# Adding expert rows to their tokens in DRAM instead of gathering them back, in a two-layer adaLN block on one Trainium2 core

## What is computed

```python
# layer 0, mixture of experts (E = 64, TOP_K = 8, SEL_K = 4)
top_val, top_idx = top_k(softmax(x @ gate_weight.T), TOP_K)
top_val = top_val / top_val.sum(-1)
mapping = where(replace, best_primary, arange(E))   # merges secondary experts
rerouted = mapping[top_idx]
rerouted[:, :SEL_K] = top_idx[:, :SEL_K]
y = silu(gate) * up @ down            # per expert, rows of its tokens
out = zeros.at[tok].add(y * w)        # back to the tokens
x = x + gb * out
# layer 1, attention (16 heads, 4 kv heads, window 128, 16 meta keys)
h = layernorm(x) * (1 + ca) + sa
x = x + ga * attention(h)
```

## Time and profile before

| | us |
|---|---|
| median of 3 runs (lowest, highest) | 2322.02 (2320.09, 2323.6) |
| the profiled execution, device time | 2322.45 |
| its span in the profile | 2320.6 |
| PE busy | 2024.3 (87%) |
| DVE busy | 1095.3 (47%) |
| ACT busy | 742.9 (32%) |
| POOL busy | 725.6 (31%) |
| mean granted TensorE clock | 0.935 |
| HBM read, written | 216.47 MB, 83.36 MB |

### The profile page before, as it was taken

The page is one execution under the profiler, slowest core; times in us unless marked ns, Lnnn a source line. Parts: engine busy times, 40 slices in busy tenths (PEclk is TensorE's granted clock), DMA queues, the critical chain, the costliest instruction groups (busy, mean ns, idle before and its releaser), DMA issues. The chain is left out here.

```text
span 2320.6 us, 38481 instructions
## 1 busy us (share of the span) xinstructions
PE 2024.3 (87%) x11149; PEld 1332.4 (57%) x11150; DVE 1095.3 (47%) x2952; ACT 742.9 (32%) x1743; POOL 725.6 (31%) x1163
## 2 busy tenths in 40 slices
PE   4799867999999999999971588888866999999998
PEld 2667534555555555555531255555545878878787
DVE  2467667555553222222114577777634444443432
ACT  0233226222222222222210255555642333222322
POOL 0243311222333333333226677777402101011000
PEclk7799879999999999999985689999987999999999
DMA  6556632565555656656625222223011112121210
GB/s 239 177 211 219 235 116 65 182 214 180 190 182 196 193 191 211 215 195 199 213 94 147 82 82 76 83 79 85 5 43 40 64 55 82 64 81 63 73 64 28
DMA packets 122554, 302.32 MB, mean 130 GB/s; under 512 B 24912, under 2 KB 28624, under 8 KB 122320
## 3 DMA queue, kind: packets, MB, share of 16 engines
q1 hardware_dynamic: 73424, 179.04, 22.7%
q0 software_dynamic: 23040, 75.52, 11.4%
q10 hardware_dynamic: 25984, 46.38, 5.3%
HBM read 216.47 MB, written 83.36 MB: 129 GB/s over the span
## 5 line engine op out<-in xcount | busy, mean ns | idle before, releaser
L1166 PE MATMUL bank<-arena 128*128 x1272 | 445.5, 493 | 10.3 <-issue 9.2
L1166 PEld LDWEIGHTS bank<-arena 128*128 128x128 f32 x1272 | 229.6, 190 | 147.7 <-issue 16.9
L1183 PE MATMUL bank<-arena 96*128 x632 | 297.5, 593 | 0.0
L1287 DVE TENSOR_TENSOR arena<-bank,mod 128x512 f32<-128x512 f32 x158 | 109.3, 692 | 214.8 <-PE bank L1183 214.8
L1904 PE MATMUL bank<-x_hi,w_hi 128*128 128x512 f32 x512 | 200.8, 392 | 6.0 <-DVE x_lo L2037 6.0
L1904 PE MATMUL bank<-x_hi,w_lo 128*128 128x512 f32 x512 | 199.4, 389 | 0.0
L1904 PE MATMUL bank<-x_lo,w_hi 128*128 128x512 f32 x512 | 199.2, 389 | 0.0
L1282 DVE TENSOR_TENSOR arena<-arena,bank 128x192 f32<-128x192 f32 x159 | 56.3, 354 | 301.0 <-ACT arena L1204 300.6
L1199 ACT COPY arena<-bank 96x256 f32<-96x256 f32 x158 | 58.2, 368 | 423.8 <-issue 221.7
L1145 POOL DMA_INDIRECT arena<-h_moe,arena x160 | 158.4, 990 | 75.1 <-issue 74.2
L1144 POOL TENSOR_TENSOR arena<-neg_half 128x1 f32<-128x1 f32 x160 | 31.3, 196 | 461.9 <-PE bank L1175 461.7
(11 more groups left out here) (326 smaller groups left out, 3738.6 us busy)
## 6 DMA issues: line engine op xcount, KB each, us to landing
arena<-in_moe_up SPq DMA_DIRECT2D x64, 768.0 KB, 5.0
y_moe<-arena ACTq DMA_DIRECT2D x158, 256.0 KB, 3.1
y_moe<-mod SPq DMA_DIRECT2D x32, 1024.0 KB
ffn_arena<-in_ffn_up SPq DMA_DIRECT2D x64, 512.0 KB, 3.2
arena<-in_moe_down SPq DMA_DIRECT2D x64, 384.0 KB, 5.8
arena<-in_L_wmod SPq DMA_DIRECT2D x12, 1024.0 KB, 11.3
x_res<-in_L_attn_x SPq DMA_DIRECT2D x1, 4096.0 KB, 18.5
h_moe<-arena SPq DMA_DIRECT2D x16, 256.0 KB, 6.8
```

Of the source, the lines that this page charges most:

```text
L1166: mm = nc.tensor.matmul(psum[2 + b][:, 0:2 * FI], xgT[:, b, k], up_ring[:, bass.ds((e % RING) * UPW + k * 2 * FI, 2 * FI)], start=(k == 0) ...
L1183: mm = nc.tensor.matmul(psum[6 + b][:], hiddenT[:, b, n], down_ring[:, bass.ds((e % RING) * DOWNW + n * C, C)], start=(n == 0), stop=(n == 1))
L1287: nc.vector.tensor_tensor(y[:, b], psum[6 + b][:], mod[:, 0, 5], ALU.mult).then_inc(y_out, 1)
```

## The change

`y_moe` and the gathers from it go. Instead DRAM holds two sums, `x_sum[0]` and `x_sum[1]`. `x_sum[0]` starts as the residual stream (stored by SP in attention 1), `x_sum[1]` as zeros. After each expert tile POOL issues an indirect transfer with `compute_op=ALU.add` that adds the tile's 128 rows of 512 floats to rows of `x_sum[t % 2]`, chosen by the same indices as the gather; empty slots point at 128 spare rows. For this the weight must be in `y` already: the routing stage builds a dense table of weights per token and expert, which is stored behind each row of `h_moe` (now 576 floats a row), so that the gather brings it along; DVE copies its column (`w_read`) and multiplies it into `hidden` in the same instruction as before. `place`, `route_hot`, `route_w` and `pos_u` go.

In attention 2 SP loads the rows of both sums by plain transfers (`rows_in`, in a ring of eight), DVE adds them (`join_rows`) and takes the statistics in the middle of the turn, and the power, the normalisation and the modulation of tile y = m+3 follow in the same turn, where the tile was treated as p = m+2 one turn later before.

DRAM tensors, stores in attention 1, the weights in `choose`, the store in the routing stage:

```diff
 return psem
-        h_moe = dram("h_moe", [S, C])
-        y_moe = dram("y_moe", [SLOTS * P, C])
+        h_moe = dram("h_moe", [S + P, C + E])
+        x_sum = [dram(f"x_sum{b}", [S + P, C]) for b in range(2)]
...
-            sp.dma_start(h_moe[z * P:(z + 1) * P], h2[:, z % 2]).then_inc(h2_stored[z % 2], 16)
+            sp.dma_start(h_moe[z * P:(z + 1) * P, 0:C], h2[:, z % 2]).then_inc(h2_stored[z % 2], 16)
...
     for b in range(2):
         sp.wait_ge(h2_stored[b], 16 * NT // 2)
...
-        st.did(nc.vector.tensor_tensor(route_w[:, 2 * pair:2 * pair + 2], top[:], over(l2[:, 4], TOPK), ALU.mult))
+        st.did(nc.vector.tensor_tensor(two, two, over(l2[:, 4], E), ALU.mult))
+        st.settle()
+        for half, dense in enumerate((routed.first, routed.second)):
+            st.did(nc.vector.tensor_tensor(dense[:, pair].rearrange("p (t e) -> p t e", e=E), two, routed.multi[:, pair, half], ALU.mult))
...
+    sp.wait_ge(w_out, 2)
+    sp.dma_start(h_moe[0:S, C:].rearrange("(t p) e -> p t e", p=P), routed.second.rearrange("p i (t e) -> p (i t) e", e=E)).then_inc(w_stored, 16)
```

Routing stage, PE (the dense table is rerouted; eight transposes L932 stand ahead of it) and DVE (the table of rows):

```diff
     pe.wait_ge(eid_done, 1)
     for n in range(2):
         mm = nc.tensor.transpose(psum[0][0:1, (2 + n) * P:(3 + n) * P], gcol[:, n:n + 1], ident[:])
     mm.then_inc(eid_mm, 1)
-    pe.wait_ge(diag_done, 1)
-    nc.tensor.matmul(psum[0][:, 0:E], ones_b[0:E], diag, start=True, stop=True).then_inc(map_mm, 1)
...
-    dve.wait_ge(map_mm, 1)
-    st.did(nc.vector.tensor_copy(routed.map_row, psum[0][:, 0:E]))
     dve.wait_ge(table_mm, NT)
```

Expert tiles, POOL:

```diff
+    def add_rows(t, b):
+        wait_tile(pool, y_out, 1, t)
+        st.did(nc.gpsimd.tensor_copy(st_dst[:, b], column(t)))
+        st.settle()
+        st.did(nc.gpsimd.tensor_tensor(spare, neg_half[:], neg_half[:], ALU.add))
+        nc.gpsimd.indirect_dma_start(out=x_sum[b], out_offset=bass.IndirectOffsetOnAxis(ap=st_dst[:, b], axis=0), in_=y[:, b],
+                                     in_offset=None, compute_op=ALU.add).then_inc(y_added[b], 16)
...
             wait_tile(pool, x_in[b], 16, shift(half, -1))
-            st.did(nc.gpsimd.tensor_copy(st_tok[:, b], slot_rows[:, t:t + 1] if isinstance(t, int) else slot_rows[:, bass.ds(t, 1)]))
+            wait_tile(pool, w_read, 1, shift(t, -2))
+            st.did(nc.gpsimd.tensor_copy(st_tok[:, b], column(t)))
             st.settle()
...
+        if before is not None:
+            t, b, half = before
+            if not isinstance(t, int) or t:
+                add_rows(shift(t, -1), 1 - b)
```

Expert tiles, ACT and DVE:

```diff
-        if before is not None:
-            t, b, _ = before
-            wait_tile(act, y_out, 1, t)
-            dst = y_rows[t] if isinstance(t, int) else y_rows[bass.ds(t, 1)].rearrange("o p c -> (o p) c")
-            act.dma_start(dst, y[:, b]).then_inc(y_stored[b], 16)
...
-    def place(t):
-        hot = tile_of(route_hot, t)
-        second, pos = hot[:, SELK:], tile_of(routed.pos, t)
-        step(tt(pick[:, 0:SELK], second, routed.map_row.unsqueeze(1).to_broadcast([P, SELK, E]), ALU.mult))
-        step(nc.vector.tensor_reduce(moved, pick[:, 0:SELK], AX.X, ALU.add))
-        step(tt(second, moved.unsqueeze(2).to_broadcast([P, SELK, E]), iota_row[:].unsqueeze(1).to_broadcast([P, SELK, E]), ALU.is_equal))
-        step(tt(pick, hot, pos.unsqueeze(1).to_broadcast([P, TOPK, E]), ALU.mult))
-        step(nc.vector.tensor_reduce(pos_f, pick, AX.X, ALU.add))
-        st.did(nc.vector.tensor_copy(tile_of(pos_u, t), pos_f))
...
-            nc.vector.tensor_tensor(hidden[:, b], gate_act[:, b], psum[2 + b][:, FI:2 * FI], ALU.mult).then_inc(hidden_done, 1)
+            wait_tile(dve, w_read, 1, t)
+            nc.vector.scalar_tensor_tensor(hidden[:, b], gate_act[:, b], row_w[:, b:b + 1], psum[2 + b][:, FI:2 * FI],
+                                           ALU.mult, ALU.mult).then_inc(hidden_done, 1)
...
-            wait_tile(dve, y_stored[b], 16, shift(half, -1))
+            wait_tile(dve, y_added[b], 16, shift(half, -1))
             nc.vector.tensor_tensor(y[:, b], psum[6 + b][:], mod[:, 0, 5], ALU.mult).then_inc(y_out, 1)
+        if after is not None:
+            t, b, half = after
+            e = dve.value_load(tile_expert[0:1, bass.ds(t, 1)], min_val=0, max_val=E - 1)
+            wait_tile(dve, x_in[b], 16, half)
+            wait_tile(dve, hidden_done, 1, shift(t, -2))
+            nc.vector.tensor_copy(row_w[:, b:b + 1], xg[:, b, bass.ds(e + C, 1)]).then_inc(w_read, 1)
```

Attention 2, SP:

```diff
+    def rows_in(t):
+        if t >= XB:
+            sp.wait_ge(x_sums, t - XB + 1)
+        sp.dma_start(x_res[:, t], x_sum[0][t * P:(t + 1) * P]).then_inc(x_in[t % XB], 16)
+        sp.dma_start(xb[:, t % XB], x_sum[1][t * P:(t + 1) * P]).then_inc(x_in[t % XB], 16)
+    rows_in(0)
+    rows_in(1)
...
+            if y + 2 < NT:
+                rows_in(y + 2)
```

Attention 2, POOL:

```diff
-    def gather(t, js):
-        if t:
-            pool.wait_ge(y_sum, TOPK * (t - 1) + js[-1] + 1)
-        absorb()
-        for j in js:
-            nc.gpsimd.indirect_dma_start(out=yg[:, j], out_offset=None, in_=y_moe,
-                                         in_offset=bass.IndirectOffsetOnAxis(ap=pos_u[:, t, j:j + 1], axis=0)).then_inc(y_in[j], 16)
...
-    def turn(g, y, p, f, s, a, w):
-        if p is not None:
-            pool.wait_ge(stats, p + 1)
-            nc.gpsimd.tensor_tensor(r1[:, 1:2], st1[:, 7:8], neg_half[:], ALU.pow).then_inc(rstd, 1)
-            pool.wait_ge(xhat, p + 1)
-            st.did(mul(h, h, mod[:, 1, 1]))
-            st.settle()
-            nc.gpsimd.tensor_tensor(h, h, mod[:, 1, 0], ALU.add).then_inc(h_done, 1)
+    def turn(y, p, f, s, a, w):
         if w is not None:
             pool.wait_ge(ready, 2)
             pool.wait_ge(xhat, w + 1)
             nc.gpsimd.tensor_tensor(x_res[:, w], x_res[:, w], bo, ALU.add).then_inc(x_pre, 1)
-        if g:
-            gather(g, range(0, 3))
+        if y is not None:
+            pool.wait_ge(stats, y + 1)
+            if y:
+                pool.wait_ge(xhat, y)
+            nc.gpsimd.tensor_tensor(r1[:, 1:2], st1[:, 7:8], neg_half[:], ALU.pow).then_inc(rstd, 1)
...
-        if g:
-            gather(g, range(3, 5))
+        if y is not None:
+            pool.wait_ge(xhat, y + 1)
+            st.did(mul(h, h, mod[:, 1, 1]))
+            st.settle()
+            nc.gpsimd.tensor_tensor(h, h, mod[:, 1, 0], ALU.add).then_inc(h_done, 1)
```

Attention 2, DVE:

```diff
+    def join_rows(t):
+        dve.wait_ge(x_in[t % XB], 32 * (t // XB + 1))
+        nc.vector.tensor_tensor(x_res[:, t], x_res[:, t], xb[:, t % XB], ALU.add).then_inc(x_sums, 1)
...
-        if p is not None:
-            dve.wait_ge(rstd, p + 1)
-            dve.wait_ge(stats, p + 1)
-            if p:
-                dve.wait_ge(hT_mm, p)
-            nc.vector.tensor_scalar(h, x_res[:, p], st1[:, 6:7], r1[:, 1:2], ALU.subtract, ALU.mult).then_inc(xhat, 1)
...
         if y is not None:
-            for j in range(0, 3):
-                add_expert(y, j)
+            join_rows(y)
+            statistics(y)
...
         if y is not None:
-            for j in range(3, 5):
-                add_expert(y, j)
+            dve.wait_ge(rstd, y + 1)
+            dve.wait_ge(stats, y + 1)
+            if y:
+                dve.wait_ge(hT_mm, y)
+            nc.vector.tensor_scalar(h, x_res[:, y], st1[:, 6:7], r1[:, 1:2], ALU.subtract, ALU.mult).then_inc(xhat, 1)
...
-        if y is not None:
-            for j in range(5, TOPK):
-                add_expert(y, j)
-        if y is not None:
-            statistics(y)
```

162 lines of the change are left out of this document (92 added, 70 removed).

## The result

The changed kernel takes 2425.37 us (median of 4 runs, 2402.4 to 2431.68) against 2321.06: ratio 1.0431, 95% interval [1.0358, 1.0503]. It is slower by 104 us where 54 less was forecast. The profiled execution took 2430.61 us with a span of 2428.8.

A forecast was written before the change was run, and what follows sets the result against it. PE was taken to bound the expert tiles, a chain between engines attention 2. Attention 2 -112, expert tiles +49, routing +6, attention 1 +1.4, stage end +2.4: -53, rounded to -54, from 2322.45 to 2268 us; range 2200 to 2368.

The forecast's parts named there:

- First q product: Attention 2: without gathers ahead, the last weight lands sooner and the product starts at 1233, not 1246.59: -13.5 us.
- Steady turns: Attention 2: ten turns without gathers and adds go from 27.4 to 21.7 us each: -57 us.
- First four turns: Attention 2: 109 us shrink to 17, 17, 18 and 20.5 us, together 72.5: -36.5 us.
- The turn without expert work: Attention 2: a 23.3 us turn that gathers and adds nothing, 21.3 without its wait, taken as yardstick for the rest.
- attention 2 gets less: Rival: another wait replaces `h` in attention 2, turns stay at 24.5 us, 30 less gained, total 2298; chance 0.10.
- Routing and attention 1: Routing: more matmuls and copies, +6 us (+3 to +10); attention 1: small DVE instructions, +1.4 us.
- the loop: Expert tiles: `y`, addition on POOL, gather behind it, PE, next `y` but one; 6.6 us plus landing for two tiles.
- I take L as 4.2 [...]: 10.8 us for two tiles, 5.4 a tile: Expert tiles: L, the gather's landing, rises from 3.6 to 4.2 us; period 5.03 to 5.4, stage +49 us.
- The other arm of the loop: Expert tiles: `y` of g waits for the addition of g-2, which would need 8 us to land; costed at nothing.
- the addition decides: Rival: expert tiles' addition takes 1.5 to 2.0 us on POOL, or L exceeds 5; period 6.0, total 2361; chance 0.23.
- The gain from `place`: Expert tiles: `place` slows the first 30 tiles to 5.33 us from 5.03; removing it ends that penalty, 10 us.
- The traffic's upper bound: Expert tiles: an addition holds the DMA engines at most as long as a store and a gather together, 32.6%.

The follow-up runs named there:

- e6: Changed kernel with attention 2's statistics, power, normalisation and modulation back in their old places: 2440.7 us, ratio 1.044; attention 2 416.6 against 415.0 us.
- e1: Changed kernel with the accumulating transfer left out, its wait and index copy kept: 2227.1 us, ratio 0.961 to the kernel before.
- e5: Changed kernel whose addition moves only the first 64 of a row's 512 floats, with 128 descriptors as before: 2337.7 us, ratio 1.009 to the kernel before.
- e3: Changed kernel with each addition issued one tile later on POOL, behind the gather: 2315.6 us, ratio 0.999 to the kernel before.
- e12: Kernel before the change, with PE's two register loads moved to the turn's start: 2312.3 us, ratio 0.996 to the kernel before.

## Why the prediction was wrong

- **Attention 2: right** in sum (-112 against -112.7) and nearly so in its parts. First q product: -13.5 forecast, -13.0 measured (33.3 to 20.3 us into the stage). Steady turns: 21.7 forecast, 21.3 measured, over eleven turns -64 where -60 was forecast. First four turns: 72.5 forecast, 74.2 measured (1454.42 to 1528.57; 107.2 before), -33 in place of -36.5. That these two misses cancel is luck; neither is large. The turn without expert work was the right yardstick. The diff's second half, the move ahead, was in the sum at 0.4 us a turn for the later order; e6 shows that it does nearly nothing either way. The rival "attention 2 gets less" fell.
- **Routing and attention 1: right in sign.** +3.9 (forecast +6, within +3 to +10) and +3.0 (+1.4).
- **Expert tiles: the loop was right, its size wrong.** The failed step is the term "I take L as 4.2 [...]: 10.8 us for two tiles, 5.4 a tile". It measured 12.9. Of the 2.1 us too few, 0.4 are POOL (the addition takes 1.59 us where the forecast had 0.99; the small steps around it are 0.2 shorter than summed), 0.25 the leg with the down product, behind a late register load and at times at the half clock, and 1.46 the wait from gather to transposes. There the median landing of the stage was met exactly and was the wrong quantity. 0.51 of the 1.46 are the mean landing above the median, 4.71 us, with 7.9 at most; the warning stood in the earlier trace rows: 7.4 at most. The other 0.95 the sum put at nothing: it let PE transpose the rows the moment they land. In 52 of 130 tiles PE came 2.2 us after them, held up by the tile before. The forecast followed one tile's loop by itself, and there are two, which meet on PE; so a late landing can be paid by both. That the additions are the cause is shown by e1, that their bytes lengthen this leg by e5 (mean landing 3.80 us, leg 4.56); the part of the two loops is read from the trace and has no experiment of its own.
- **The other arm of the loop** (the addition's landing before the `y` after next): nothing in the changed kernel, as forecast. It becomes the next wait as soon as the addition goes behind the gather (e3).
- **The end of the stage:** +2.4 forecast, +4.2 measured (from the last `y` to the next stage 14.7 us, before 10.5).
- **The rival that came true** is "the addition decides", by its first condition, 1.5 to 2.0 us on POOL (1.59). The second, L over 5, did not hold: the landing is 4.2 in the median and 4.7 in the mean. It gave 6.0 a tile and 2361; measured are 6.42 and 2425. It was priced with the same sum over one loop, and so the range built on it ended at 2368, 57 us too low.
- **A slip in that rival** made it look farther off. "It turns slower than before when the period passes 5.75, that is when addition plus landing together rise by 1.3 us over what I took": 5.75 a tile are 11.5 for two, and that is 0.7 above the 10.8 that I took (1.3 above the 10.2 with today's landing). The addition's 0.60 us more on POOL was nearly enough by itself, so "slower" deserved more than 0.22.
- **The gain from `place`** was booked for the wrong reason: e12 gets those 9.5 us in the kernel before, with `place` still in it.
- **The traffic's upper bound was a little low:** "above by a store and a gather together, 32.6%" of 5.03 us is 1.64 us a tile; the addition takes 1.86. The bound meant as the far end was passed.

## What to carry to other kernels

When a change puts one transfer ahead of another in an engine's queue, write down what the second one now waits for, and if the chain closes on itself, compare it with the bound engine's time by its late rounds, not by the median, and count what a late round does to the other tiles that share the engine. Here order and early loads gave back 198 us; taking away seven eighths of the addition's bytes gave 88. Before giving up an accumulating transfer, issue it behind the loads that the next tiles need, check that the buffer it reads is not wanted again before it lands (e3), and move register loads ahead of the waits: the same additions then made the kernel 4.1% faster than before (2227 against 2323 us) in place of 4.3% slower. Read a change that has a gain and a loss by stages; the halves of this one were -113 and +214 us.
